# An attention and mixture-of-experts layer on one core: expert outputs scattered back by token, and a reordered start

## The reference

```python
x = layernorm(x + attention(x))   # 16 heads, 4 key/value heads of 128
x = layernorm(x + experts(x))     # 8 experts of width 176, the best 2 for each token
```

## Time and profile before

| | |
|---|---|
| device time, median of 3 runs | 990.01 us (987.09 to 993.39) |
| profiled execution | 990.93 us, of which the span from first to last instruction is 989.0 us |
| PE busy | 924.6 us (93%) |
| DVE, ACT, POOL busy | 643.2 (65%), 661.8 (67%), 620.6 (63%) |
| mean granted TensorE clock | 0.979 of full speed |
| HBM read, written | 25.52 MB, 18.35 MB |

### The profile page before, as it was taken

The page is one execution under the profiler, slowest core; times in us unless marked ns, Lnnn a source line. Parts: engine busy times, 40 slices in busy tenths (PEclk is TensorE's granted clock), DMA queues, the critical chain, the costliest instruction groups (busy, mean ns, idle before and its releaser), DMA issues.

```text
span 989.0 us, 18166 instructions
## 1 busy us (share of the span) xinstructions
PE 924.6 (93%) x5332; PEld 720.6 (73%) x5332; DVE 643.2 (65%) x1483; ACT 661.8 (67%) x2139; POOL 620.6 (63%) x612
## 2 busy tenths in 40 slices
PE   3899999999999999999999999999999989999870
PEld 2767787878777777878778787877777766777650
DVE  4676767676767676767676969676887664321164
ACT  4777777777777777777777777776667664455442
POOL 6658775767565657677767667776658880230374
PEclk9899999999999999999999999999999999999995
DMA  7101100000000000700000000010102121343444
GB/s 247 33 17 33 39 1 1 6 12 6 1 0 0 0 0 7 256 7 1 1 2 1 1 7 6 1 62 2 62 1 78 38 84 42 96 134 102 139 139 148
DMA packets 35648, 44.88 MB, mean 45 GB/s; under 512 B 3568, under 2 KB 29552, under 8 KB 35440
## 3 DMA queue, kind: packets, MB, share of 16 engines
q1 hardware_dynamic: 32496, 35.50, 11.3%
q0 software_dynamic: 3072, 8.39, 2.7%
HBM read 25.52 MB, written 18.35 MB: 44 GB/s over the span
## 4 chain that ended last, share of the span: by engine, by line
PE 84%; ACT 5%; DVE 5%; issue 3%; POOL 1%; another core or an unknown queue 1%; DMA 0%; POOLq 0%; DVEq 0%; ACTq 0%; SPq 0%
PE OA L560 13%; PE PR L461 13%; PE S L513 11%; PE MS L533 9%; PE S L542 7%; PE OA L522 5%; PE S L659 5%; PE OA L676 4%; PE OA L553 4%; PE PR L489 3%; PE PR L485 3%; ACT eqk L788 2%; PE MS L474 1%; PE S L504 1%; PE MS L564 1%
## 5 line engine op out<-in xcount | busy, mean ns | idle before, releaser
L1439 POOL TENSOR_TENSOR qd<-eqk,eg 128x512 f32<-128x512 f32 x63 | 74.8, 1187 | 165.4 <-issue 156.5
L560 PE MATMUL OA<-wT,V 128*128 128x512 f32 x320 | 148.4, 594 | 0.0
L750 ACT ACTIVATE S<-S,nm 128x128 f32<-128x128 f32 (+3 forms) x256 | 126.8, 495 | 25.8 <-DVE nm L965 22.5
L788 ACT ACTIVATE eqk<-qkv,nmx 128x128 f32<-128x128 f32 x320 | 124.3, 396 | 6.9 <-DVE nmx L1040 6.4
L965 DVE TENSOR_REDUCE nm<-S 128x2 f32<-128x256 f32 (+3 forms) x128 | 102.0, 817 | 28.0 <-PE S L513 24.8
L1427 POOL TENSOR_TENSOR eqk<-eqk,rse 128x640 f32<-128x640 f32 x63 | 79.9, 1267 | 52.7 <-DVE rse L1083 28.0
L560 PEld LDWEIGHTS OA<-wT,V 128*128 128x128 f32 x320 | 59.5, 190 | 69.4 <-issue 68.9
L999 DVE TENSOR_TENSOR pr<-S,rl 128x256 f32<-128x256 f32 (+3 forms) x128 | 105.5, 825 | 5.3 <-DVE rl L995 0.3
L1416 POOL TENSOR_TENSOR rp<-qkv,cos 128x640 f32<-128x640 f32 x64 | 99.5, 1554 | 7.2 <-ACT qkv L778 7.0
L1419 POOL TENSOR_TENSOR rp<-rp,rt 128x640 f32<-128x640 f32 x64 | 99.5, 1554 | 5.0
L1416 POOL TENSOR_TENSOR rt<-qkv,sin 128x640 f32<-128x640 f32 x64 | 99.1, 1548 | 0.0
(11 more groups left out here) (164 smaller groups left out, 2495.9 us busy)
## 6 DMA issues: line engine op xcount, KB each, us to landing
qkv<-slot_x SPq DMA_DIRECT2D x46, 128.0 KB
slot_y<-eqk SPq DMA_DIRECT2D x46, 128.0 KB
gu_w<-in_wgu SPq DMA_DIRECT2D x8, 352.0 KB, 3.6
slot_x<-zero SPq DMA_DIRECT2D x2, 1280.0 KB, 7.3
stage<-in_wqkv SPq DMA_DIRECT2D x6, 384.0 KB, 3.3
xraw<-in_x_cols SPq DMA_DIRECT2D x16, 128.0 KB, 2.3
acc<-in_x_rows SPq DMA_DIRECT2D x1, 2048.0 KB, 11.5
dn_w<-in_wdn SPq DMA_DIRECT2D x8, 256.0 KB, 4.2
```

Source lines behind the costliest of these rows:

```text
L560: last = pe.matmul(OA[:, :], V[:, j, :], wT[:, j, :], start=(c == 0 and j == 0), stop=(j == c))
L750: nc.scalar.activation(S[:, h, 0:n], S[:, h, 0:n], ACT.Exp, bias=nm[:, h:h + 1], scale=1.0, accum_out=ls[:, h:h + 1]).then_inc(s_exp, 1)
L788: last = nc.scalar.activation(eqk[:, par, h * 128:(h + 1) * 128], qkv[:, c % C, h * 128:(h + 1) * 128], ACT.Exp, bias=nmx[:, h:h + 1], sca ...
```

## The change

Three things change.

1. A sorted row is 258 numbers wide instead of 256 (`ROW`). The first extra one is the token's number less 8192, copied from a table into `acc` once; the second is the number of the token's best expert, written by `slots`. When a tile's rows have been loaded, DVE's `way_back` makes from them the row of `plane` where each result belongs: token, plus 2048 if the tile's expert is the token's second, or out of range for padding. `send_back` on GpSimd scatters the finished tile there with a bounds test. `plane` holds first choices and second choices in token order, so `load_rows` on SP reads both with one plain load, where `fetch` gathered. `yo` has five buffers. SP issues no stores of tiles.
2. GpSimd's order changes with it: the late norms, the sends of the second set and the powers stand between the scatters; `load_slots(q)` also waits for `way_back(q - 4)`.
3. The start: the first projection uses whole float32 input and weights (`project_whole`) and doesn't wait for the split; eleven matmuls of zeros come before it and four in two later places (`keep_warm`); the memsets go from GpSimd to DVE; GpSimd waits for DVE's `decay(0, 0)` before it splits x tile 2 and rotates tile 1; ACT does the gate logs before the features, and `features(0, 1)` before `q_out(0, 0)`; SP issues x tiles 2 and 3, the first jobs and `acc` after the first projection.

The core of the diff (not shown: `acc[..., BODY]` in place of `acc[..., :]`, and the tables):

```diff
+ROW = HID + 2
+YO = 5
+NOWHERE = 8192.0
...
             sp.dma_start(wTf, wo_in[:, 0:2048]).then_inc(s_wor, 16)
+            sp.wait_ge(s_proj, 1)
             load_x(0, 2)
...
                 later(sp, s_tx, q - 3)
+                later(sp, s_back, q - 3)
                 sp.dma_start(xg[:, q % 4, :], slot_rows(slot_x, q)).then_inc(s_xg[q % 4], 16)
...
-            def store_slots(q):
-                sp.wait_ge(s_yo, q + 1)
-                sp.dma_start(slot_rows(slot_y, q), yo[:, q % 3, :]).then_inc(s_y[q % 3], 16)
+            def load_rows(t):
+                if t == 0 or t == SETS[1][0]:
+                    for i in range(YO):
+                        sp.wait_ge(s_y[i], stored(NT_A if t == 0 else NT, i))
+                later(sp, s_cb, t - 3)
+                sp.dma_start(yg[:, t % 4, :, :], plane.rearrange("(r m) n -> m r n", r=2)[t * P128:(t + 1) * P128]).then_inc(s_yg[t % 4], 16)
...
+            for q in range(3, NT):
+                load_slots(q)
+                if q >= 38:
+                    load_rows(q - 38)
+            for t in range(NT - 38, TILES):
+                load_rows(t)
...
+            still = zero[:, 0:HID].bitcast(BF16)
+            def keep_warm(n):
+                for _ in range(n):
+                    pe.matmul(OA[:, :], still[:, 0:P128], still[:, :], start=True, stop=True)
+            def project_whole():
+                pe.wait_ge(s_xr[0], 16)
+                for k in range(KT2):
+                    pe.wait_ge(s_w0[k], 16)
+                    for a, b in ((0, 512), (512, QKV)):
+                        last = pe.matmul(PR[:, a:b], xraw[:, 0, k, :], prf[:, k * QKV + a:k * QKV + b],
+                                         start=(k == 0), stop=(k == KT2 - 1))
+                last.then_inc(s_proj, 1)
...
-            pe.wait_ge(s_splo, 1)
-            project(0, 0, lambda: pe.wait_ge(s_splo, 2))
+            pe.wait_ge(s_tab, 1)
+            keep_warm(11)
+            project_whole()
+            pe.wait_ge(s_splo, 2)
+            project(0, 1)
             pe.wait_ge(s_cst, 64)
-            project(0, 1)
             gate_sums(0, 0)
-            turn(0, 0, True)
+            keep_warm(4)
+            turn(0, 0, True, lambda: keep_warm(4))
...
             copy_out(0, 0)
+            gate_logs(0, 0)
             features(0, 0)
-            gate_logs(0, 0)
             copy_out(0, 1)
             exp_gates(0, 0)
+            features(0, 1)
             q_out(0, 0)
-            features(0, 1)
...
+                if r == 0:
+                    link(nc.vector.tensor_tensor(prod, one, cm[:, tile_at + 1:tile_at + 1 + E].rearrange("p (o e) -> p o e", o=1)
+                                                 .to_broadcast([P128, m, E]), ALU.mult))
+                    link(nc.vector.tensor_reduce(acc[:, a:b, ROW - 1], prod, AX_X, ALU.add))
...
+            def way_back(q):
+                dve.wait_ge(s_xg[q % 4], 16 * (q // 4 + 1))
+                if q == 0 or q == NT_A:
+                    dve.wait_ge(s_te, 1 if q == 0 else 2)
+                second = backf[:, q % 2:q % 2 + 1]
+                nc.vector.tensor_scalar(second, xg[:, q % 4, ROW - 1:ROW], tef[:, q:q + 1], float(B * N),
+                                        ALU.not_equal, ALU.mult).then_inc(s_bf, 1)
+                dve.wait_ge(s_bf, q + 1)
+                nc.vector.scalar_tensor_tensor(out=back[:, q:q + 1], in0=xg[:, q % 4, HID:HID + 1], scalar=NOWHERE, in1=second,
+                                               op0=ALU.add, op1=ALU.add).then_inc(s_back, 1)
...
                 if q < NT:
                     multiply(q)
+                    way_back(q)
...
-            def fetch(t):
...
+            def send_back(q):
+                pool.wait_ge(s_yo, q + 1)
+                pool.wait_ge(s_back, q + 1)
+                nc.gpsimd.indirect_dma_start(plane, bass.IndirectOffsetOnAxis(ap=back[:, q:q + 1], axis=0),
+                                             yo[:, q % YO, :], None, bounds_check=2 * B * N - 1, oob_is_err=False).then_inc(s_y[q % YO], 16)
...
+            pool.wait_ge(s_qd, 2)
+            x_wait(0, 2)
+            x_split(0, 2)
             rotate(0, 1)
...
+            nc.gpsimd.tensor_copy(acc[:, :, HID], marks).then_inc(s_mark, 1)
...
+            norms = {0: (12, 14), 1: (14, 15), 2: (15, 16)}
+            sends = {14: 12, 15: 13, 16: 14, 17: 15}
+            deviations = {36 + 2 * i: (i // 2, i % 2) for i in range(5)}
+            for q in range(NT):
+                for t in range(*norms.get(q, (0, 0))):
+                    norm1(t)
+                send_back(q)
+                if q in sends:
+                    send(sends[q])
+                if q in deviations:
+                    rs2(*deviations[q])
+            rs2(2, 1)
             rs2(3, 0)
             rs2(3, 1)
```

More of the change, by code:

```diff
@@ L78, in tri, with layer_kernel @@
     return c * (c + 1) // 2
-def layer_kernel(nc, x_rows, x_cols, wqkv, wo_in, wgu, wdn, gate, rope_cos, rope_sin, cmat, cmask, slot_x, slot_y, out):
+def layer_kernel(nc, x_rows, x_cols, wqkv, wo_in, wgu, wdn, gate, rope_cos, rope_sin, cmat, cmask, slot_x, plane, out):
     with ExitStack() as ctx:
@@ L102, in layer_kernel @@
         stage = sb("stage", [P128, 2, WJOB], F32)
-        acc = sb("acc", [P128, TILES, HID], F32)
+        acc = sb("acc", [P128, TILES, ROW], F32)
         cos = sb("cos", [P128, C, D], F32)
@@ L254, in layer_kernel @@
         s_th, s_hT, s_dn, s_yo, s_pad = (sem(n) for n in ("s_th", "s_hT", "s_dn", "s_yo", "s_pad"))
-        s_y = [sem(f"s_y{i}") for i in range(3)]
+        s_y = [sem(f"s_y{i}") for i in range(YO)]
+        s_mark, s_back, s_bf = sem("s_mark"), sem("s_back"), sem("s_bf")
         s_yg = [sem(f"s_yg{i}") for i in range(4)]
@@ L314, in stored @@
         def stored(q, s):
-            return 16 * len([i for i in range(q) if i % 3 == s])
+            return 16 * len([i for i in range(q) if i % YO == s])
         def wq_cols(t, kv, k, a, b):
@@ L343, in acc_tile @@
             if isinstance(t, int):
[L344 to L345 removed]
+                return acc[:, t, BODY]
+            return acc[:, bass.ds(t, 1), BODY].rearrange("p o n -> p (o n)")
         def kv_count(g, c):
@@ L475, in gate_sums, with turn @@
                 pe.matmul(MS[:, 128:130], gl[:, :], halves, start=True, stop=True).then_inc(s_g, 1)
-            def turn(g, c, has_next):
+            def turn(g, c, has_next, between=None):
                 u = C * g + c
@@ L486, in turn @@
                 last.then_inc(s_trq, 1)
+                if between:
+                    between()
                 pe.wait_ge(s_qd, 2 * (u + 1))
@@ L882, in y_out @@
                 act.wait_ge(s_dn, q + 1)
-                later(act, s_y[q % 3], 16 * (q // 3))
-                nc.scalar.copy(yo[:, q % 3, :], OA[:, 0:HID]).then_inc(s_yo, 1)
+                later(act, s_y[q % YO], 16 * (q // YO))
+                nc.scalar.copy(yo[:, q % YO, :], OA[:, 0:HID]).then_inc(s_yo, 1)
             def norm2(n, i):
-                a = acc[:, TPB * n + i, :]
+                a = acc[:, TPB * n + i, BODY]
                 act.wait_ge(s_nmr, 2 * n + i // 2 + 1)
@@ L1101, in norm_stats @@
             def norm_stats(which, t):
-                nc.vector.bn_stats(st[which][:, t % TPB, :], acc[:, t, :]).then_inc(s_bn[which], 1)
+                nc.vector.bn_stats(st[which][:, t % TPB, :], acc[:, t, BODY]).then_inc(s_bn[which], 1)
             def moments(t):
@@ L1328, in shift2 @@
                                                op0=ALU.mult, op1=ALU.mult).then_inc(s_nmr, 1)
+            nc.vector.memset(zero[:, :], 0.0).then_inc(s_tab, 1)
+            nc.vector.memset(neghalf[:, :], -0.5)
+            for e in range(E):
+                if e:
+                    nc.vector.memset(tri8[:, e, 0:e], 1.0)
+                nc.vector.memset(tri8[:, e, e:E], 0.0)
+            nc.vector.memset(ones[:, :], 1.0).then_inc(s_tab, 1)
             for i in range(KT2):
@@ L1357, in _ @@
             multiply(0)
+            way_back(0)
             add_output(NG - 1, C - 1)
@@ L1525, in rs2 @@
                 nc.gpsimd.tensor_tensor(rstd[2][:, i], ve[2][:, i], neghalf[:, i], ALU.pow).then_inc(s_rs[2], 1)
-            for c in range(3):
+            for c in range(2):
                 x_wait(0, c)
                 x_split(0, c)
-            nc.gpsimd.memset(neghalf[:, :], -0.5).then_inc(s_tab, 1)
-            for e in range(E):
-                if e:
-                    nc.gpsimd.memset(tri8[:, e, 0:e], 1.0)
-                last = nc.gpsimd.memset(tri8[:, e, e:E], 0.0)
-            nc.gpsimd.memset(ones[:, :], 1.0)
-            last = nc.gpsimd.memset(zero[:, :], 0.0)
-            last.then_inc(s_tab, 1)
             pool.wait_ge(s_cst, 64)
             rotate(0, 0)
+            pool.wait_ge(s_qd, 2)
+            x_wait(0, 2)
+            x_split(0, 2)
             rotate(0, 1)
```

73 lines of the change are left out of this document (27 added, 46 removed).

## The result

The changed kernel takes 980.26 us (median of six, 978.83 to 980.99), the kernel before 990.0 on the same chip: ratio 0.990, 95% interval 0.988 to 0.992. The profiled execution took 980.99 us with a span of 979.2, against 989.0. So 9.8 us of span went, where my sum had 15.2.

The account below looks back on a forecast made before the run. TensorE, 84% of the chain, was taken as the bound, leaving the start, expert-tile waits and the end: -9.4 + 0.7 - 4.5 - 2.0 = -15.2 us on a 989.0 span gave 973.8, or 974.8 against the median; range 966 to 984.

Parts of the forecast that it names:

- The start, -9.4: Start: earlier first projection and uncontended DVE products bring the rotation of tile 2 from 35.94 to 26.5; bounds 6.0 to 10.5.
- this load: Start: load of the whole input tile `acc`, which DVE awaits before its first step; forecast to land at 21.4 us.
- 25.8 and 26.5: Start: forecast times of tile 2's rotation, by GpSimd's own work (25.8) and by the input load's path (26.5).
- The product of 0.29 us: Start: time taken for one DVE product with GpSimd idle, so five run alone would take 1.5 us, not 5.94.
- Routing, +0.7: Routing: two more DVE operations in `slots` on the chain cost 0.7 us (0 to 1.0).
- The expert tiles, -4.5: Expert stage: scatters hide and the gathers' bursts go, gaining 4.5 us (0 to 7).
- the second stretch: Expert stage before, 948.41 to 956.80: two tiles lost 3.4 us, half of it left to ACT's norms.
- The end, -2.0: After the last output copy: 21.4 us instead of 23.4, last scatter 2.5 us late; gain 2.0 us (-1 to 4).
- (b): Rival, expert tiles: scatters become the bound, at 2.9 us each adding 33 us; total 1012 us; chance 0.08.
- (c): Rival, start: another load or the `acc` wait (landing later than 28) takes the whole gain; 986 to 989; chance 0.07.
- (a): Rival: half the gain; clock stays low in first projection (gain 6.0), expert stalls cost as now; 982.7 us; chance 0.19.

Follow-up runs that it names:

- in its own run: Only the changed kernel's start (zero matmuls, whole-float first projection, new engine order, memsets on DVE) put into the kernel before: 979.4 us, ratio 0.993.
- the eleven executions: Profiled executions of the changed kernel and its variants that have both the zero matmuls and GpSimd's new wait; rotation of tile 2 starts at 26.55 to 27.46 us.
- by their own run: Changed kernel with three output buffers, not five: 979.0 us, ratio 0.991, loss beside the sends 8.0 us.
- by its own run: Changed kernel with the powers rs2(2, 0) moved behind the last output scatter: 976.6 us, ratio 0.989; 19.8 us from last copy to end, not 21.7.

## Why the forecast was right in sign and 5.5 us too good

**The start, -9.4: right, measured -9.2 at the first output copy, -8.8 in its own run.** The copy was even earlier than forecast (8.8, not 9.5), the clock rose, the wait made the products short, though 2.73 and not 1.5 us, for a reason I had not seen: the first rotation waits for the mask. The claim that is only half true is "What is late next is therefore this load, not GpSimd". In the profiled execution GpSimd was the later one, and with the load out of the way the rotation of tile 2 stayed; in five of the eleven executions it was the load. Both paths were nearly equal, as I had worked out (25.8 and 26.5), and both were longer by a little: 11.0 us from the split to the rotation, not 10.1, and 5.26 from the score maximum, not 4.9. So the number hung little on the choice; that it came within 0.2 us is in part luck, as the gain at the rotation was 8.9 and the first output copy came anywhere between 830.28 and 832.43 in these executions.

Three small readings behind it were off. The product of 0.29 us was not one with GpSimd idle: GpSimd starts an operation 0.05 us into it, at 27.90. Five products that begin 0.4 us before GpSimd's rotation ends take 1.68 to 1.70 us together. At the low clock the copy would have ended at 11.3 + 0.81 = 12.1, not 12.2. And eighteen memsets moved, not seventeen.

**Routing, +0.7: not visible.** The two operations take 0.26 and 0.26 us for the first set, 0.5 together; from the step at 50 to 60 us, which ran 8.9 us earlier, to the first output copy, 9.2 earlier, nothing was lost.

**The expert tiles, -4.5: measured +1.2, outside the term's own bounds of 0 to 7 us of gain. This step failed**, and in it one sentence: "While four tiles each carry three scatters (3.8 us), GpSimd falls behind by 5 us; five output buffers allow 12.4 us, so ACT doesn't wait". The count is right (scatter 16 went out 3.4 us late), the buffers do hold (three would do, by their own run), and still ScalarE waited, for TensorE. I had priced the interleaving by GpSimd's time and by buffers, and left the 2.2 us that the sends lost in the kernel before as they were; the changed kernel makes of a run of eight DMAs one of twelve, and the loss went from 2.2 to 10.5. The trace of before held the hint: the stalls of the earlier trace rows fell by time on bursts, I took the gathers' bursts out of the account, and did not ask which new burst the change makes. The other part of the term was too small: I left half of the second stretch to ScalarE's norms, and it went whole, 3.25 + 3.9 = 7.1 us at the upper bound.

**The end, -2.0: measured -1.7**, with the last scatter 2.7 us late as forecast, and shown by its own run to be on the path.

**The rivals.** (b) did not come: the scatter takes 0.97 us, 1.11 at most, beside DVE's work. The Trainium skill (SBUF — State Buffer, "Who interferes with whom") has DVE and GpSimd lock each other out on a shared port; here that shows in DVE's products beside GpSimd (5.50 us against 1.7), not in the time that GpSimd takes to issue. (c) wanted a load that lands later than 28; the score maximum had its rows at 21.34. (a), with 982.7, is nearer to the measured 980.3 than the forecast is, but not by its mechanism: the start gave 9.2 us and not 6.0, and both stretches of the earlier trace rows went. It had the right worry, that scattering keeps that queue busy, and the wrong place: scatters alone, one per tile, cost nothing in 50 us.

**What stays open** is the path by which a run of GpSimd's DMAs reaches TensorE. The trace can't say whether TensorE worked late or only its signals came late: its own instructions stand at their usual times up to 879.02, while all that waits for them is 2 to 8 us late. It is shown that the stall comes with the packed DMAs, moves with them, and goes neither with the buffers nor, for the sends, with the rows in each. That it is the length of the run that counts, and not the DMAs per tile, is only argued.

## What to carry to other kernels

When work is moved to GpSimd's indirect DMAs, count the longest run without a pause, not only the time of each: here four scatters in a row were free where a pause followed, and twelve DMAs cost 8 to 10.5 us of an engine that had nothing to do with them. Spread such DMAs so that a pause of some 1.4 us comes after every third, which cost nothing here, and look for the deadline on the other side (a load that waits for the last of them). Where two paths end within a microsecond, as in this start, take the gain of removing one as nothing until both are moved.

## What the runs showed of the hardware that I had not expected

What the other engines await from TensorE comes late beside runs of GpSimd's indirect DMAs, from about the fifth on, at a DMA share of only 0.36. And the start of the same program differs between executions: eleven zero matmuls from 1.18 us on took 3.85 to 4.88 us, that is, the clock rose at different times, which moved the start of the first copy between 7.87 and 9.18 and the rotation of tile 2 by 0.9 us at most. Kernels with gathers spread more from run to run than those without: by 6.3 us (987.1 to 993.4) for the kernel before and 8.8 (978.1 to 986.9) with the new start alone, and by at most 3.2 in every kernel without gathers. That the gathers' stalls vary is seen in two traces (3.25 and 4.9 us at copies 33 to 36); that they make the spread is only argued.
